# Reciprocals of the softmax row sums ahead of the older item's context on VectorE, in the steps of items 3 to 27

## The reference

```
scores = q @ k.T / sqrt(32);  scores = scores * mask - 10000 * (1 - mask)
probs  = softmax(scores);     context = probs @ v
stream = stream + context @ w_o + b_o
```

## Time and profile before

| what | us |
| --- | --- |
| median of three runs | 1094.88 |
| the profiled execution's own time | 1093.23 |
| its span, from the first to the last instruction | 1091.8 |
| TensorE busy | 1066.6 (98%) |
| VectorE busy | 823.3 (75%) |
| ScalarE busy | 703.4 (64%) |
| GpSimd busy | 483.8 (44%) |

### The profile page before, as it was taken

One profiled execution on the slowest core, in us unless ns is written; L12 is line 12 of the kernel. 1 busy time (PEld: TensorE's weight loads), 2 busy tenths in 40 slices (PEclk: granted clock), 3 DMA queues, 4 the chain that ended last, 5 costly groups with the idle time before them and its releaser, 6 DMA issues.

```text
span 1091.8 us, 24224 instructions
## 1 busy us (share of the span) xinstructions
PE 1066.6 (98%) x8741; PEld 924.8 (85%) x8741; DVE 823.3 (75%) x1303; ACT 703.4 (64%) x2354; POOL 483.8 (44%) x361
## 2 busy tenths in 40 slices
PE   8999999999999999998999999999999999999998
PEld 7888888888888888887898888888888988888886
DVE  8678877777878788888867667767697466666767
ACT  5677877777788788786444444444456276666676
POOL 4665566567777776767513122114032222222310
PEclk9999999999999999999999999999999999999999
DMA  7356665577677777564243151341647636766621
GB/s 247 99 181 208 193 205 173 185 215 232 212 220 219 219 218 228 174 197 133 87 144 107 59 174 52 123 143 56 208 135 266 218 128 205 211 203 208 203 67 60
DMA packets 145927, 185.92 MB, mean 170 GB/s; under 512 B 17952, under 2 KB 88848, under 8 KB 145808
## 3 DMA queue, kind: packets, MB, share of 16 engines
q1 hardware_dynamic: 145808, 184.37, 54.1%
HBM read 122.59 MB, written 61.73 MB: 169 GB/s over the span
## 4 chain that ended last, share of the span: by engine, by line
PE 59%; DVE 13%; ACT 10%; POOL 7%; issue 5%; DMA 4%; SPq 2%; DVEq 0%; ACTq 0%; POOLq 0%
PE psum L1094 15%; PE psum L1075 14%; PE psum L897 13%; POOL prob L2244 6%; PE psum L889 5%; PE psum L1014 5%; ACT prob L1399 4%; ACT prob_blocks L1399 2%; PE psum L915 2%; DVE ln_tile L1720 2%; DVE prob L1785 2%; DVE negmax L1798 2%; DMA ln_tile<-stream 2%; PE psum L991 2%; ACT inputs_transposed L1437 1%
## 5 line engine op out<-in xcount | busy, mean ns | idle before, releaser
L897 PE MATMUL psum<-inputs_hi,weights_hi 128*128 128x256 f32 x768 | 223.7, 291 | 3.0 <-ACT kT L1350 1.5
L897 PE MATMUL psum<-inputs_lo,weights_hi 128*128 128x256 f32 x768 | 217.1, 283 | 0.0
L897 PE MATMUL psum<-inputs_hi,weights_lo 128*128 128x256 f32 x768 | 216.9, 282 | 0.0
L2244 POOL TENSOR_TENSOR prob<-prob,mask_bias 128x1024 f32<-128x1024 f32 x64 | 152.6, 2406 | 98.6 <-DVE prob L1785 98.1
L897 PEld LDWEIGHTS psum<-inputs_hi,weights_hi 128*128 128x128 f32 x768 | 146.7, 191 | 8.4 <-ACT kT L1350 2.0
L1798 DVE TENSOR_REDUCE negmax<-prob 128x8 f32<-128x1024 f32 x96 | 115.6, 1211 | 50.1 <-POOL prob L2244 50.0
L1399 ACT ACTIVATE prob<-prob,negmax 128x128 f32<-128x128 f32 x384 | 148.2, 390 | 0.1
L897 PEld LDWEIGHTS psum<-inputs_lo,weights_hi 128*128 128x128 f32 x768 | 147.0, 191 | 0.2
L897 PEld LDWEIGHTS psum<-inputs_hi,weights_lo 128*128 128x128 f32 x768 | 146.9, 191 | 0.0
L2230 POOL TENSOR_TENSOR inputs_lo<-inputs_transposed,inputs_hi 128x512 fp32r<-128x512 f32 x70 | 93.4, 1355 | 91.0 <-DVE inputs_hi L1758 58.9
L1399 ACT ACTIVATE prob_blocks<-prob,negmax 128x128 f32<-128x128 f32 x304 | 117.5, 388 | 22.1 <-DVE negmax L1798 22.1
(11 more groups left out here) (137 smaller groups left out, 2657.2 us busy)
## 6 DMA issues: line engine op xcount, KB each, us to landing
weights_whole<-weights_in SPq DMA_DIRECT2D x80, 256.0 KB, 3.7
prob_turned<-prob_blocks SPq DMA_DIRECT2D x38, 512.0 KB, 3.0
prob<-prob_turned SPq DMA_DIRECT2D x152, 128.0 KB, 3.4
inputs_transposed<-normalised SPq DMA_DIRECT2D x120, 128.0 KB, 2.9
normalised<-ln_tile SPq DMA_DIRECT2D x24, 512.0 KB, 2.8
context<-row_sums_spread SPq DMA_DIRECT2D x188, 64.0 KB, 2.1
stream<-residual SPq DMA_DIRECT2D x42, 256.0 KB, 2.9
ln_tile<-stream SPq DMA_DIRECT2D x32, 256.0 KB, 3.9
```

Of the source, the lines that this page charges most:

```text
L897: mm = pe.matmul(ps[:, bank, GT * part:GT * part + GT], w[:, slot, c, o], a[:, buf, c, :], start=c == 0 and i == 0, stop=c == KC - 1 and i ...
L2244: pool.tensor_tensor(half, half, mb.unsqueeze(1).to_broadcast([128, 8, T]), ALU.add).then_inc(s_biased, 1)
```

## The change

`inverse_sums(g-1)` moves on VectorE ahead of the two halves of `context(g-2)` in the steps of items 3 to 27. No instruction is added or taken away, no other engine's program is touched, and steps 0 to 2 and 28 on keep their order.

```diff
                 if g - 1 in WHOLE:
                     inverse_sums(g - 1)
                     turn_second_blocks(g - 1)
+                ahead = g in range(3, 28)
+                if ahead:
+                    inverse_sums(g - 1)
                 if st.ends and not late:
                     context(g - 2, 0)
                     context(g - 2, 1)
                 if st.ends and not late and phase == D:
                     make_mask_bias(g)
                     mask_scores(g, 0)
-                if st.ends and not late and g - 1 not in WHOLE:
+                if st.ends and not late and not ahead and g - 1 not in WHOLE:
                     inverse_sums(g - 1)
```

## The result

The changed kernel took 1103.15 us (median of four runs, 1102.95 to 1106.26) beside 1094.09 for the kernel before in the same session: a ratio of 1.009, 95% interval 1.0074 to 1.0105, so 8 to 11.5 us slower. Run again among the experiments it gave 1.0095 (1.0080 to 1.0111). The forecast was 1106.0, +11.2 us; the sign and the size hold: the medians are 9.1 us apart, and the ratios give +9.8 and +10.4.

The account below looks back on a forecast made before the run. Softmax chain over VectorE, GpSimd and ScalarE bounds it, TensorE in steps 12 to 16. 4.5 + 1.5 + 4.8 + 0.4 = 11.2 us on 1093.23 gives 1104.4, plus 1.65 for the median: 1106.0 us, range 1101.0 to 1108.5.

Parts of the forecast that it names:

- The bound: Steps 3 to 11 and 17 on: softmax chain sets the pace, not TensorE; at most 2.3 us to gain.
- Odd steps: Contexts fall behind the reciprocal's wait for the last exponential; last sum to first mask 1.85 us instead of 1.02.
- A pair of steps in A: Odd plus even step, steps 3 to 10: costs 0.86 + 0.26 = 1.12 us, four pairs 4.5 us.
- steps 11 to 17: TensorE has slack here; chain walked by leads and rigid parts makes it 6.0 us late, 1.5 more than at step 11.
- Even steps: Reciprocal, hidden by VectorE's wait for ScalarE's high part, is no longer hidden: all behind it 0.23 us later, 0.26 after waiting.
- Phase B: Steps 17 to 27: a pair takes 30.5 us instead of 29.3, +1.15; together 4.8 us.
- the pair 21 to 23: A DMA sets the pace, a 1.36 us wait in step 22, and hides all but 0.2 us of the cost.
- Steps 28 to 31: Old order kept, but item 27's masks are further behind; 0.4 to 0.5 us reaches TensorE at step 31.
- Rival (c): Steps 17 to 27 held by DMAs, each pair costing 0.3 us there: 7.5 us, 1102.4; chance 15%.
- (a): TensorE binds and gets reciprocals sooner in steps 19, 23, 25, 27: 1.4 us faster, 1093.5; chance 4%.
- (b): Masks' delay falls into slack of ScalarE or GpSimd inside the rigid spans: no change, 1094.9; chance 4%.
- TensorE's waits: Waits for reciprocals about 1.5 us in odd steps 3 to 11 and 17 to 27; first-stretch idle 0.7 to about 5.

Follow-up runs that it names:

- experiment 3: Kernel before, its order kept, but in odd steps 3 to 27 VectorE waits for the last exponential ahead of the contexts: 1099.76 us, ratio 1.0060.
- experiment 7: Against the kernel before, reciprocals moved ahead of the contexts in steps 19, 23, 25 and 27 alone: 1096.86 us, ratio 1.0020.
- experiment 8: Against the kernel before, VectorE in odd steps 3 to 27 does contexts, two masks, reciprocal, low parts, two masks: 1096.96 us, ratio 1.0023.
- experiment 6: Against the kernel before, reciprocals moved ahead of the contexts in steps 12 to 27 alone: 1098.28 us, ratio 1.0044.
- experiment 1: Against the kernel before, reciprocals moved ahead of the contexts in the 13 odd steps 3 to 27 alone: 1100.1 us, ratio 1.0061.

## Why the prediction was right

*The bound* was read rightly. TensorE's 98% did not set the pace of steps 3 to 11 and 17 to 27; the softmax chain over VectorE, GpSimd and ScalarE did. Experiments 3 and 7 show it from both sides: reciprocals 0.67 us later for TensorE with the same loss as the move, and in step 23 reciprocals 0.92 sooner of which 0.15 is left one step later. One sentence of this part was wrong: that no edit could gain more in these steps than TensorE's idle time, 2.3 us. With the masks ahead (experiment 8) TensorE came to step 11 1.8 us sooner, where its idle time in that stretch had been 0.67: busy time holds waiting too.

*Odd steps: the contexts pushed behind a wait.* Right in place and form. Predicted lead 1.85 us, measured 1.72. The term was mis-sized in its own time of the reciprocal: I set 0.26, its duration, between its start and that of the contexts; the rows show 0.17 where it waited and 0.15 where it didn't. Contexts to masks take 1.52 instead of 1.56, since the pair of contexts is 0.69 long and not 0.74. The lead grew by 0.70 and not by 0.86. A pair of steps in A costs 0.76 (3.02 / 4) and not 1.12. This alone is 1.5 of the 2.1 us by which the forecast was over, and part of the miss in steps 11 to 17 (0.9 for 1.5), whose walk used the same leads.

*Even steps: no longer hidden.* Right in mechanism, over in size: 0.11 for 0.23 (and 0.26 in the price of a pair); in B the lead of the even steps grew by 0.20 for 0.30 (1.66 to 1.86). A duration in a row is not the time to the next start; the next instruction began before the reciprocal's end.

*Phase B*: +4.1 for +4.8 in steps 17 to 28. The pairs are 30.2 us, one 30.55 (375.36 to 405.91), for 30.5: the lead is 1.86 in odd and even steps, and not 1.99. That the pair 21 to 23 would pay little, since a load held it, is what the second trace shows, and more: 30.24 after 30.83, less than before even, where +0.2 was forecast. In the first trace these steps cost +5.6.

*Steps 28 to 31*: +0.5 for +0.4. *Rival (c)*, B held by loads, gave 1102.4, near the measured 1103.2, but for a wrong reason: experiment 6 has B and the seam alone at +4.8. *Rivals (a) and (b)* fell with experiments 7 and 1. (The 25 us of idle time on VectorE that (b) was given are 117.0 - 93.70 = 23.3.)

*TensorE's waits* were forecast wrong. They were to rise to about 1.5 us in the odd steps, and its idle time in the first stretch to 5. The rows have 0.44 in steps 3 to 11, as before, and 0.2 to 0.8 in 17 to 27. The loss is there, in the distance of the steps, but most of it is booked as TensorE's busy time. The signs to look at were the leads and the distances.

*Some luck.* The second trace ends 11.1 us after that of before, next to the forecast of 11.2. But 1.5 of it came before step 3 and 1.1 after step 31, where the change does nothing and the trace shows a lower clock (last section). Between them it is 8.5 us, and 12.9 in the first trace. The medians, 9.1 apart, lie between. Why the same program takes 4.4 us more between these steps in one execution than in another stays open, but for the two places in steps 13 and 14 named with the traces.

## What to carry to other kernels

On an in-order engine a move ahead carries the moved instruction's wait to all that it is moved past; ask of those whether they were ready in that idle time, and who stands behind them. A wait on the busiest engine is worth removing only if the chain that feeds it is not the one that sets the pace: compare its next arrival, one step later. Idle time before a wait is where work that is ready belongs, but check what runs on the neighbour engine at the new place.

## What the hardware showed that was not expected

- VectorE's low part (two inputs in SBUF, 128x256) took 0.76 us for a pair while GpSimd was idle and 2.80 while GpSimd's bias ran (161.39 to 163.78), experiment 8; in all 13 odd steps of that trace it took 2.64 to 2.89. The masks, with one input in PSUM, show no such cost: before the change four of them take 2.47 to 2.48 us with the bias beside the last of them (149.06 in step 8), and two take 1.27 in experiment 8 without it.
- A reciprocal of 16 columns lasts 0.23 to 0.26 us in its row, and an independent instruction behind it starts 0.15 to 0.17 after its start.
- TensorE's granted clock was 1.00 throughout the profiled execution of before and not in most others. First the second trace of the changed kernel, then the same two places in the trace of before, at the start and at the seam of phase B and the MLP:

```profile
10.00:20.00 10.00, 9.08 (x44) 7.77 (x44) 9.04 (x14) 5.12 (x9) 4.43 (x5) 0.83 1.04 374
505.00:520.00 15.00, 12.67 (x92) 10.58 (x91) 11.84 (x17) 9.87 (x38) 7.95 (x7) 0.89 0.40 133
```

```profile
10.00:20.00 10.00, 9.14 (x57) 8.29 (x58) 9.04 (x14) 5.81 (x11) 4.43 (x5) 1.00 1.04 380
505.00:520.00 15.00, 13.96 (x92) 10.68 (x91) 13.25 (x16) 8.01 (x16) 12.70 (x9) 1.00 0.49 157
```

A mean under 1.00 means that a part of it ran at 1.2 GHz and not 2.4: here for about 3.4 us each time, from 11.4 and from 513.1. Ahead of both TensorE had been idle, busy 0.08 us from 10 to 11 and 0.19 from 510 to 512. In the trace of before it was as idle at both places (0.14 us from 10 to 11, 0.18 from 500 to 502) and kept its clock. The six traces with 0.83 between 10 and 20 us are the six in which step 3 comes 1.4 to 1.6 us late; in the six others, with 1.00 there, before among them, it is 0.8 us late or less. The clock is no part of the change, the fastest kernel's trace has both places too, and it makes up much of the spread of 1090 to 1098 us: of 26 runs of before in one session the 11 with a mean clock of 1.000 took 1092.6 us on average, the 10 with 0.998 took 1094.8, and the 5 with 0.997 took 1096.0. So two kernels that are 1 or 2 us apart are best compared among runs with the same clock.
